# An adaptive-gate FFN with a quantised second layer on one core: GpSimd takes part of VectorE's and ScalarE's work, and the first FFN slots are put in a new order

## The chip, the cores and the metric

One core of one Trainium2 chip. The metric is the device time of one execution in microseconds. TensorE is called PE, VectorE DVE, ScalarE ACT, GpSimd POOL and SyncE SP below.

## The reference, cut to what matters

x holds 8 row blocks of 128 x 512 in float32. Layer 0 gates x and runs a ternary FFN on it; layer 1 multiplies by a weight that is first quantised with a codebook, and then by a base matrix with low-rank experts.

```python
y = einsum('bet,bt->be', x, mask) / length            # masked row means: x_sum, y_mean
g = x * sigmoid(conv5(y))                             # conv, y_safe, gates
aq = round(g * 127 / rowmax(|g|))                     # x_max, x_scales, x_quantise
wq(w) = clip(round(w / mean|w|), -1, 1) * mean|w|     # weight_sum, weight_total, ternary
h = silu(aq @ wq(w_gate).T) * (aq @ wq(w_up).T)       # gate_up, hidden_chunk
x = x + act_quant(h) @ wq(w_down).T                   # hidden_scale, down, residual
delta = lora_B @ lora_A * 0.5
q = codebook[searchsorted(thresholds, (weight + delta) / scale)]
w_eff = q * scale + delta                             # normalise, masks, codebook, value, w_eff
z = x @ w_eff.T
x = x + z @ W_base.T + b + sum_e alpha_e * (z @ A_e.T) @ B_e.T * 2
```

## The kernel before

Every engine has a program written out by hand; the order in it is the order on the engine, and counting semaphores join them. There is no scheduler.

**Codebook stage.** The 512 x 512 weight lies in four tiles of 128 rows (k = 0 to 3) in `cond`. ACT scales a tile by the inverse scale (`scaled_weight`, four instructions), DVE adds the low-rank delta (`normalise`), makes seven 0/1 tiles `w > threshold` (`masks`, 128 x 512 each), and PE multiplies each by a diagonal of codebook steps and adds them up in PSUM (`codebook`). DVE multiplies by the scale (`value`) and adds the delta again (`w_eff`, 128 x 512 from two SBUF tiles). PE then folds w_eff and W_base together into one matrix M: `fold(o, k)` adds row tile o's part of column block k to `bank_m[k]`, 16 folds in all, which end in `m_copy` on ACT.

**Weights of the FFN.** ACT sums |w| of each part that lands (`weight_sum`), PE adds over the partitions (`weight_total`), DVE turns it into a scale (`weight_scale`), ACT rounds a chunk of columns to int16 (`rounded_chunk`), DVE clips it to -1, 0 or 1 (`ternary_chunk`). There are three chunks of 464, 464 and 448 columns, for gate (i = 0) and up (i = 1). The down weight has five parts; ACT sums three and DVE two.

**Slots.** A loop b = 0 to 7 runs on PE, ACT and DVE. Slot b holds `gate_up(b, 0..2)`, the two products of row block b by a chunk; ACT makes silu of the first, DVE multiplies by the second (`hidden_chunk`: a product and a row maximum), then `hidden_scale` gives the factor hq(b). ACT rounds (`hidden_round`), SP transposes by DMA, ACT evacuates (`hidden_evacuate`), and `down(b)` multiplies two or three slots later; `residual(b)`, `x1_transposes(b)` and `x1_low(b)` follow. gate_up of chunk n needs hidden_chunk n - 2 done, which frees the bank. The row blocks form groups 0 to 1, 2 to 4 and 5 to 7: sums, the conv, gates and scales are made for a group at a time, inside the slots. `last_fold`, `b_rows` and the low part of `m_s` (DVE, line 1373) are small steps of layer 1 that `x1_transposes(0)` waits for in slot 3. Behind slot 7 comes layer 1 proper.

**Loads.** SP issues all of them in one order, first the head: 1060 columns of 4 bytes on 128 partitions, which hold the low-rank pair of layer 1's weight (1024 columns) and small numbers (codebook, lengths, active experts, log scales).

## Time and profile before

| | us |
|---|---|
| median of 3 runs | 153.93 (153.88 to 154.12) |
| the profiled execution | 153.92 |
| its span, first to last instruction | 152.1 |
| PE, DVE, ACT, POOL busy | 138.4, 114.1, 96.1, 11.0 |

Busy time is what an engine spent in instructions; matmuls overlap at their ends, so PE's is a little high. An instruction's cost on its engine is best read as the distance from its start to the next one's when nothing is waited for. A bracket at the end of a row gives the idle time ahead of it and what ended that. Idle time costs something only on the engine that the others wait for.

### The profile page before, as it was taken

Reading aid. Unit: us, or ns where it says so; the run is one execution under the profiler, and the core shown is the slowest. Engines: PE = TensorE matmul, PEld = TensorE weight load, DVE = VectorE, ACT = ScalarE, POOL = GpSimd, SP = SyncE. Lnnn points to the kernel's source line nnn. Section 1 sums busy time; section 2 is a strip of 40 time slices with the busy share of each in tenths; the row PEclk is TensorE's granted clock in tenths of the full one; section 3 lists DMA queues with packets and bytes.
Section 4 is the critical chain, followed back from the end, with each engine's and each line's share of the span. In section 5 each row is a group of like instructions: output and inputs, shape, how many; then the busy total and the mean of one; then the engine's idle time right before and its main releaser. Section 6 shows DMA issues by size and latency. Waiting matters only on the chain.

```text
span 152.1 us, 2134 instructions
## 1 busy us (share of the span) xinstructions
PE 138.4 (91%) x661; PEld 84.7 (56%) x661; DVE 114.1 (75%) x302; ACT 96.1 (63%) x156; POOL 11.0 (7%) x31
## 2 busy tenths in 40 slices
PE   6779999998799967898579999999999999999993
PEld 2256665753356544446234545454576766797792
...
DMA packets 19486, 19.22 MB, mean 126 GB/s; under 512 B 13474, under 2 KB 13858, under 8 KB 19476
## 3 DMA queue, kind: packets, MB, share of 16 engines
...
## 4 chain that ended last, share of the span: by engine, by line
PE 50%; DVE 27%; ACT 10%; issue 8%; DMA 2%; SPq 0%; ACTq 0%; DVEq 0%
PE bank L971 15%; PE bank L918 12%; ACT tern_d L526 6%; PE bank L881 6%; PE bank L887 6%; DVE hmax L1322 5%; DVE raw_gate L1319 4%; PE bank L929 3%; DVE junk L1158 2%; DMA cond<-in_cond_w 2%; DVE rmax L1208 2%; ACT cond L492 2%; PE bank L978 1%; DVE tern_i L1203 1%; PE bank L863 1%
## 5 line engine op out<-in xcount | busy, mean ns | idle before, releaser
L881 PE MATMUL bank<-tern_g,head_sb 128*128 128x464 bf16 (+1 forms) x96 | 22.6, 357 | 1.0 <-DVE tern_u L1204 0.8
L887 PE MATMUL bank<-tern_u,head_sb 128*128 128x464 bf16 (+1 forms) x96 | 22.5, 357 | 0.6 <-DVE raw_gate L1319 0.6
L918 PE MATMUL bank<-tern_d,delta 128*128 128x512 bf16 (+1 forms) x88 | 22.0, 399 | 0.5 <-DVE tern_d L1204 0.5
L971 PE MATMUL bank<-m_h,fr 128*128 128x512 f32 (+1 forms) x72 | 22.3, 378 | 0.0
L1319 DVE TENSOR_TENSOR raw_gate<-bank,wbt 128x464 f32<-128x464 f32 (+1 forms) x24 | 15.1, 631 | 4.2 <-ACT wbt L624 3.7
L624 ACT ACTIVATE wbt<-bank,s_g 128x464 f32<-128x464 f32 (+1 forms) x24 | 14.9, 633 | 3.4 <-PE bank L881 3.3
L1322 DVE TENSOR_REDUCE hmax<-raw_gate 128x1 f32<-128x464 f32 (+1 forms) x24 | 15.1, 631 | 0.8
L631 ACT ACTIVATE raw_gate<-raw_gate,hq 128x1376 int16<-128x1376 f32 x8 | 11.5, 1438 | 6.5 <-DVE hq L1329 6.5
L918 PEld LDWEIGHTS bank<-tern_d,delta 128*128 128x128 bf16 (+1 forms) x88 | 9.0, 103 | 11.5 <-issue 1.9
L887 PEld LDWEIGHTS bank<-tern_u,head_sb 128*128 128x128 bf16 x96 | 9.3, 98 | 10.0 <-DVE raw_gate L1319 1.2
L796 PE MATMUL bank<-wbt,cond 128*128 128x512 f32 x32 | 14.8, 599 | 0.0
L971 PEld LDWEIGHTS bank<-m_h,fr 128*128 128x128 f32 x72 | 13.2, 189 | 2.7
L785 PE MATMUL bank<-masks,diag_h 128*128 128x512 f32 x28 | 12.4, 444 | 1.9 <-DVE masks L1120 1.9
L881 PEld LDWEIGHTS bank<-tern_g,head_sb 128*128 128x128 bf16 x96 | 8.8, 101 | 8.8 <-DVE tern_u L1204 1.3
L971 PE MATMUL bank<-m_l,fr 128*128 128x512 f32 (+1 forms) x36 | 13.3, 370 | 0.0
L1120 DVE TENSOR_SCALAR masks<-cond,th 128x512 fp32r<-128x512 f32 x28 | 11.7, 483 | 0.2
L786 PE MATMUL bank<-masks,diag_l 128*128 128x512 f32 x28 | 11.1, 395 | 0.0
L1341 DVE TENSOR_TENSOR fr<-bank,fr 128x512 fp32r<-128x512 f32 x8 | 5.5, 692 | 7.2 <-ACT fr L658 7.0
L464 POOL TENSOR_SCALAR head_sb<-xs,gate,qx 128x512 int16<-128x512 f32 x6 | 5.4, 897 | 70.6 <-DVE qx L1224 69.2
L658 ACT ACTIVATE fr<-bank 128x512 fp32r<-128x512 f32 x8 | 4.7, 594 | 8.0 <-PE bank L929 8.0
L1432 DVE TENSOR_TENSOR xs<-bank,xs 128x512 f32<-128x512 f32 (+1 forms) x9 | 5.2, 625 | 5.8 <-PE bank L978 5.8
L796 PEld LDWEIGHTS bank<-wbt,cond 128*128 128x128 f32 x32 | 5.8, 190 | 5.5 <-issue 5.0
...
## 6 DMA issues: line engine op xcount, KB each, us to landing
...
```

The costliest lines, as they stand in the source:

```text
L624: act.activation(silu[:, n % 2, 0:w], bank_g[n % 2][:, 0:w], ACT.Silu, scale=s_g[:, b:b + 1]).then_inc(silu_done, 1)
L631: act.activation(h_i[:, b % 2, 0:F], hbuf[b % 2], ACT.Copy, scale=hq[:, b:b + 1]).then_inc(hint_done, 1)
L785: pe.matmul(bank_cb[k][:], diag_h[:, t, :], mask[i % SLOTS], start=(n == 0), stop=False)
L786: mm = pe.matmul(bank_cb[k][:], diag_l[:, t, :], mask[i % SLOTS], start=False, stop=(n == NT - 1))
L796: mm = pe.matmul(bank_m[k][:], cond[:, o, k * P:(k + 1) * P], wbt[:, o, :], start=(o == 0), stop=(o == KH - 1))
L881: mm = pe.matmul(bank_g[n % 2][:, 0:w], xq_t[:, b % 2, k, :], tern_g[:, k, f0:f0 + w], start=(k == 0), stop=(k == KH - 1))
L887: mm = pe.matmul(bank_u[n % 2][:, 0:w], xq_t[:, b % 2, k, :], tern_u[:, k, f0:f0 + w], start=(k == 0), stop=(k == KH - 1))
L918: mm = pe.matmul(bank_down[:], h_t[0:rows, b % 2, j, :], tern_d[0:rows, j, :], start=(j == 0), stop=(j == KF - 1))
L971: pe.matmul(bank_y[n_res][:, h0:h1], a[:, b, k, :], m[:, k, h0:h1], start=(n == 0), stop=False)
L1120: dve.tensor_scalar(mask[i % SLOTS], cond[:, k, :], t(T_ORDER[n]), None, ALU.is_gt)\
L1319: dve.tensor_tensor(hs, bank_u[n % 2][:, 0:w], silu[:, n % 2, 0:w], ALU.mult)\
L1322: link(dve.tensor_reduce(hmax[:, b % 2, c:c + 1], hs, AX.X, ALU.max, apply_absolute_value=True))
```

## The change

- **Head.** The small numbers (36 columns) become a transfer of their own, issued by ACT; the pair of 1024 columns stays first on SP's queue. The thresholds are put in order and the lengths and expert numbers made ahead of `normalise(0)`, which now waits for ACT's scaled groups one at a time.
- **GpSimd.** It scales tiles 1 to 3 (three 128 x 512 products, in place of twelve ACT instructions), makes all four `w_eff`, and for row blocks 5 to 7 makes the 0/1 mask and its product with x; ACT sums that product (`masked_sum`, at the end of slot 2). DVE's three `x_sum` of these blocks go.
- **Down weight.** DVE sums three parts instead of two.
- **Hidden scale.** The maxima of chunks 0 and 1 lie behind the hidden row, and the reduction of chunk 2 takes them in; the separate reduction goes.
- **Order.** The folds of tile 1 to 3 go from between the codebooks into the waits ahead of slot 0 and into slots 0 and 1; the ternary chunks are made as listed in ROUNDED, gate and up by turns; row block 2 is transposed by DMA, block 1 on PE ahead of slot 0. Only `m_copy` 3 and 2 are left; 1 and 0 stay in PSUM. Silu of chunk (b+1, 0) is issued in slot b for b up to 3. The weight total of the down weight goes behind gate_up(2, 1), selection_out ahead of hidden chunk (1, 2), and in slot 3 residual and m_s go ahead of hidden chunk (3, 1).

```diff
-X_BY_DMA = 3
+X_BY_DMA = 2
...
+ROUNDED = ((0, 0), (0, 1), (1, 0), (1, 1), (0, 2), (1, 2))
+SILU_TO = 4
+M_ORDER = (3, 2, 1, 0)
+M_COPIED = 2
...
-SUMMED_BY_ACT = 3
...
+SUMMED_BY_ACT = 2
...
-            sp.dma_start(head_sb[:], head).then_inc(ld_head, 16)
+            sp.dma_start(head_sb[:, 0:2 * H], lora0).then_inc(ld_lora, 16)
...
+            transpose_x(2)
             for b in range(NB):
                 if b < H_BY_DMA:
                     transpose_h(b)
-                if X_BY_DMA <= b + 3 < NB:
+                if b + 3 < NB:
...
+            def scaled_weight(k):
+                pool.wait_ge(inv_done, 1)
+                pool.wait_ge(ld_cond[k], 16)
+                v = cond[:, k, :].rearrange("p (g i) -> p g i", g=KH)
+                pool.tensor_tensor(v, v, scl_inv[:, k, :].unsqueeze(2).broadcast_to([P, KH, GROUP]),
+                                   ALU.mult).then_inc(condn_done, 1)
+
+            def w_eff(k):
+                pool.wait_ge(delta_done, min(k + 2, KH))
+                pool.wait_ge(value_done, k + 1)
+                pool.tensor_tensor(cond[:, k, :], cond[:, k, :], delta[:, k, :], ALU.add).then_inc(weff_done, 1)
+
+            def masked_x(b):
+                m = masked[:, b - GROUPS[2][0], :]
+                pool.wait_ge(ld_x[b], 16)
+                pool.wait_ge(len_done, 1)
+                pool.tensor_scalar(m, t_iota[:], len_f[:, b:b + 1], None, ALU.is_lt).then_inc(below_done, 1)
+                pool.wait_ge(below_done, b - GROUPS[2][0] + 1)
+                pool.tensor_tensor(m, m, xs[:, b, :], ALU.mult).then_inc(masked_done, 1)
+
+            for k in range(1, KH):
+                scaled_weight(k)
+            w_eff(0)
+            w_eff(1)
...
+            w_eff(2)
+            w_eff(3)
+            pool.wait_ge(cb_ps, KH)
+            for b in range(GROUPS[2][0], NB):
+                masked_x(b)
...
+            act.dma_start(head_sb[:, 2 * H:HEAD], head).then_inc(ld_head, 16)
...
-            scaled_weight(0)
+            act.wait_ge(inv_done, 1)
+            act.wait_ge(ld_cond[0], 16)
+            for g in range(KH):
+                c = slice(g * GROUP, (g + 1) * GROUP)
+                act.activation(cond[:, 0, c], cond[:, 0, c], ACT.Copy,
+                               scale=scl_inv[:, 0, g:g + 1]).then_inc(condn0_done, 1)
...
+            def masked_sum(b):
+                i = b - GROUPS[2][0]
+                act.wait_ge(masked_done, i + 1)
+                act.activation(masked[:, i, :], masked[:, i, :], ACT.Copy,
+                               accum_out=ysum[:, b:b + 1]).then_inc(xsum_done, 1)
...
             weight_sum_up(0)
             weight_sum_up(1)
+            conv_out(0)
             weight_sum_up(2)
+            gate_silu(0)
+            weight_sum_up(3)
             rounded_chunk(0, 0)
-            weight_sum_up(3)
             rounded_chunk(0, 1)
-            conv_out(0)
-            rounded_chunk(0, 2)
-            gate_silu(0)
+            x_evacuate(0)
+            x_evacuate(1)
             rounded_chunk(1, 0)
-            x_evacuate(0)
             rounded_chunk(1, 1)
...
+                if b == 2:
+                    for i in range(GROUPS[2][0], NB):
+                        masked_sum(i)
...
                 fold(0, k)
             codebook(2)
             weight_total(0, bank_total[0], KH)
-            for k in range(KH):
-                fold(1, k)
+            conv(0)
             codebook(3)
-            conv(0)
             weight_total(1, bank_total[1], KH)
-            for k in range(KH):
-                fold(2, k)
...
-            fold(KH - 1, 0)
-            fold(KH - 1, 1)
+            fold(1, 0)
+            fold(1, 1)
+            fold(1, 2)
             x_transposes(0)
-            fold(KH - 1, 2)
+            x_transposes(1)
+            fold(1, 3)
+            fold(2, 3)
+            fold(2, 2)
+            fold(2, 1)
             for b in range(NB):
                 gate_up(b, 0)
+                if b == 0:
+                    fold(3, 3)
+                    fold(3, 2)
+                    conv(1)
...
-                if b == 2:
-                    weight_total(2, bank_total[2], len(DOWN_PARTS))
                 if b == 3:
                     down(0)
                     last_fold(2)
+                    conv(2)
                     last_fold(3)
                 gate_up(b, 1)
-                if b == 3:
-                    conv(2)
...
                 if b == 2:
+                    weight_total(2, bank_total[2], len(DOWN_PARTS))
                     last_fold(0)
...
                     selection(KH)
+                    fold(2, 0)
+                    fold(3, 0)
...
-            def w_eff(k):
-                dve.wait_ge(delta_done, min(k + 2, KH))
-                dve.wait_ge(value_done, k + 1)
-                dve.tensor_tensor(cond[:, k, :], cond[:, k, :], delta[:, k, :], ALU.add).then_inc(weff_done, 1)
...
+            inner_thresholds()
+            lengths()
+            outer_thresholds()
+            adapter_numbers()
             normalise(0)
-            masks(0, 0, 1)
-            ordered_thresholds()
-            masks(0, 1)
+            dve.wait_ge(th_done, 2)
+            masks(0)
             normalise(1)
             masks(1, 0, 3)
             value(0)
             masks(1, 3)
-            w_eff(0)
             normalise(2)
+            selectors()
             value(1)
-            w_eff(1)
-            masks(2)
-            lengths()
+            masks(2, 0, 4)
+            x_sum(0)
+            masks(2, 4)
+            x_sum(1)
+            y_mean(0)
...
-                link(dve.tensor_reduce(hmax[:, b % 2, c:c + 1], hs, AX.X, ALU.max, apply_absolute_value=True))
+                if c < NC - 1:
+                    row_max, src = hrow[b % 2][:, F + c:F + c + 1], hs
+                else:
+                    row_max, src = hred[:, b:b + 1], hrow[b % 2][:, f0:F + NC - 1]
+                link(dve.tensor_reduce(row_max, src, AX.X, ALU.max, apply_absolute_value=True))
...
                 if b == 1:
-                    y_reciprocal(1)
-                    gates(1)
-                    x_scales(2, 5)
+                    weight_sum_down(2)
...
-                    x_max(5, NB)
                     residual(0)
+                    dve.wait_ge(msh_done, 1)
+                    dve.tensor_tensor(ms_l, bank_ms.rearrange("p (k c) -> p k c", k=KH),
+                                      ms_h.bitcast(F32), ALU.subtract).then_inc(msl_done, 1)
...
                 if b == 1:
+                    selection_out()
                     weight_sum_down(3)
+                if b < NB:
+                    if b == 0:
+                        y_reciprocal(1)
+                        gates(1)
+                        x_scales(1)
+                    hidden_chunk(b, 2)
+                    if b == 3:
+                        residual(1)
+                    hidden_scale(b)
+                if b == 1:
                     weight_sum_down(4)
-                if b < NB:
-                    hidden_chunk(b, 2)
-                    hidden_scale(b)
-                if b == 0:
-                    x_max(2, 5)
-                if b == 1:
                     weight_scale(2, bank_total[2])
-                    selection_out()
...
                     ternary_down(4)
-                    x_sum(5)
-                    x_sum(6)
-                    x_sum(7)
+                    dve.wait_ge(xsum_done, NB - GROUPS[2][0])
                     y_mean(2)
-                if b == 3:
-                    y_reciprocal(2)
-                    gates(2)
-                    x_scales(5, NB)
-                    x1_low(0)
-                if 3 <= b <= NB + 1:
+                    x_max(5, 6)
+                    x_max(6, 7)
```

GpSimd ahead of the slots, before: five iotas and small steps up to `fold_two` (line 444 on), then nothing until it quantises rows of x (line 464).

```order
L442 MEMSET ones 128x128
L444 TENSOR_SCALAR low_row<-part 128x1
L445 TENSOR_SCALAR tmp_row<-part 128x1
L447 TENSOR_TENSOR low_row<-low_row,tmp_row 128x1
L449 TENSOR_SCALAR sign_row<-low_row 128x1
L450 TENSOR_SCALAR two_row<-part 128x1
L453 TENSOR_SCALAR fold_two<-diff 128x36
L454 TENSOR_SCALAR fold_tmp<-diff 128x36
L456 TENSOR_TENSOR fold_two<-fold_two,fold_tmp 128x36
L464 TENSOR_SCALAR head_sb<-xs,gate,qx 128x512 x2
```

And now: the scalings (line 461), two w_eff (line 467), the same small steps, the other two w_eff.

```order
L455 MEMSET ones 128x128
L461 TENSOR_TENSOR cond<-cond,scl_inv 128x512 x3
L467 TENSOR_TENSOR cond<-cond,delta 128x512 x2
L482 TENSOR_SCALAR low_row<-part 128x1
L483 TENSOR_SCALAR tmp_row<-part 128x1
L485 TENSOR_TENSOR low_row<-low_row,tmp_row 128x1
L487 TENSOR_SCALAR sign_row<-low_row 128x1
L488 TENSOR_SCALAR two_row<-part 128x1
L491 TENSOR_SCALAR fold_two<-diff 128x36
L492 TENSOR_SCALAR fold_tmp<-diff 128x36
L494 TENSOR_TENSOR fold_two<-fold_two,fold_tmp 128x36
L467 TENSOR_TENSOR cond<-cond,delta 128x512 x2
```

The seven instructions on `cond` are new on this engine, and the small steps have moved behind five of them; the masks and products (lines 473 and 475) follow.

PE from the weight total of the up weight to slot 0's second chunk, before. `wbt,cond` are folds, `ident_b,head_sb` transposes of x, `tern_g` and `tern_u` the two halves of gate_up.

```order
L757 MATMUL bank<-wsum,ones 128x4
L796 MATMUL bank<-wbt,cond 128x512 x6
L853 MATMUL bank<-ident_b,head_sb 128x128 x4
L796 MATMUL bank<-wbt,cond 128x512
L881 MATMUL bank<-tern_g,head_sb 128x464 x4
L887 MATMUL bank<-tern_u,head_sb 128x464 x4
L881 MATMUL bank<-tern_g,head_sb 128x464 x4
L887 MATMUL bank<-tern_u,head_sb 128x464 x4
L796 MATMUL bank<-wbt,cond 128x512
L815 MATMUL bank<-ymean,band 128x3
L853 MATMUL bank<-ident_b,head_sb 128x128 x4
L881 MATMUL bank<-tern_g,head_sb 128x448 x4
```

And now, over the same stretch:

```order
L810 MATMUL bank<-wsum,ones 128x4
L849 MATMUL bank<-wbt,cond 128x512 x3
L901 MATMUL bank<-ident_b,head_sb 128x128 x8
L849 MATMUL bank<-wbt,cond 128x512 x4
L932 MATMUL bank<-tern_g,head_sb 128x464 x4
L938 MATMUL bank<-tern_u,head_sb 128x464 x4
L849 MATMUL bank<-wbt,cond 128x512 x2
L868 MATMUL bank<-ymean,band 128x3
L932 MATMUL bank<-tern_g,head_sb 128x464 x4
L938 MATMUL bank<-tern_u,head_sb 128x464 x4
L849 MATMUL bank<-wbt,cond 128x512
L932 MATMUL bank<-tern_g,head_sb 128x448 x4
```

Seven folds stand ahead of gate_up(0, 0) as before, but they are four of tile 1 and three of tile 2 in place of four of tile 2 and three of tile 3; both transposes come ahead of the last four; tile 3's first two folds stand behind gate_up(0, 0).

DVE from the end of slot 2 into slot 3, before. `xs<-bank` is residual(0), `m_s` the low part that x1_transposes(0) waits for.

```order
L1203 TENSOR_SCALAR tern_i<-raw_down,winv 96x512
L1204 TENSOR_SCALAR tern_d<-tern_i 96x512
L1158 SCALAR_TENSOR_TENSOR junk,ysum<-t_iota,len_f,xs 128x512 x3
L1163 TENSOR_TENSOR ymean<-ysum,len_r 128x3
L1319 TENSOR_TENSOR raw_gate<-bank,wbt 128x464
L1322 TENSOR_REDUCE hmax<-raw_gate 128x1
L1208 TENSOR_REDUCE rmax<-xs 128x3
L1336 SCALAR_TENSOR_TENSOR xs<-bank,s_d,xs 128x512
L1319 TENSOR_TENSOR raw_gate<-bank,wbt 128x464
L1322 TENSOR_REDUCE hmax<-raw_gate 128x1
L1373 TENSOR_TENSOR m_s<-bank,m_s 128x4x36
```

And now:

```order
L1262 TENSOR_SCALAR tern_i<-raw_down,winv 96x512
L1263 TENSOR_SCALAR tern_d<-tern_i 96x512
L1222 TENSOR_TENSOR ymean<-ysum,len_r 128x3
L1267 TENSOR_REDUCE rmax<-xs 128x1 x2
L1387 TENSOR_TENSOR raw_gate<-bank,wbt 128x464
L1394 TENSOR_REDUCE raw_gate<-raw_gate 128x1
L1408 SCALAR_TENSOR_TENSOR xs<-bank,s_d,xs 128x512
L1430 TENSOR_TENSOR m_s<-bank,m_s 128x4x36
L1387 TENSOR_TENSOR raw_gate<-bank,wbt 128x464
L1394 TENSOR_REDUCE raw_gate<-raw_gate 128x1
```

The three masked sums on `junk` are gone, two of the three maxima of x (`rmax`) stand ahead of the first hidden product, and `m_s` stands ahead of the second hidden product instead of behind it.

## Rows read from the trace of the kernel before

**Rows 1.** The page: shares of the span in the chain that ended last, by engine.

```profile
PE 50%; DVE 27%; ACT 10%; issue 8%; DMA 2%; SPq 0%; ACTq 0%; DVEq 0%
```

**Rows 2.** Busy time of each engine in three stretches, instructions in brackets; then clock, DMA.

```profile
50.00:55.00 5.00, 3.69 (x25) 2.48 (x24) 4.62 (x14) 4.29 (x8) 1.50 (x2) 1.00 0.38 72
75.00:80.00 5.00, 2.98 (x10) 1.56 (x11) 3.93 (x12) 2.56 (x5) 0.00 (x0) 0.72 0.00 0
90.00:95.00 5.00, 5.00 (x29) 2.75 (x28) 2.47 (x5) 5.00 (x9) 0.00 (x0) 1.00 0.41 79
```

**Rows 3.** VectorE's instructions in order of time, head and codebook stage.

```profile
1.09 0.23 DVE L1068 TENSOR_SCALAR ident<-diff 128x128 f32<-128x128 f32 x1
...
1.23 0.63 DVE L1069 TENSOR_SCALAR ident_b<-diff 128x128 bf16<-128x128 f32 x1
4.13 0.16 DVE L1073 TENSOR_REDUCE cbm<-head_sb 128x1 f32<-128x8 f32 x1 [2.26 <-DMA head_sb<-in_head]
...
6.29 1.13 DVE L1108 SCALAR_TENSOR_TENSOR cond<-bank,inv_part,cond 128x128 f32<-128x128 f32 x4 [0.45 <-ACT cond L492]
...
17.59 0.75 DVE L1128 SCALAR_TENSOR_TENSOR cond<-bank,cbn,scl 128x512 f32<-128x512 f32 x1 [0.16 <-DVE cond L1108]
18.45 0.69 DVE L1135 TENSOR_TENSOR cond<-cond,delta 128x512 f32<-128x512 f32 x1
19.05 2.86 DVE L1120 TENSOR_SCALAR masks<-cond,th 128x512 fp32r<-128x512 f32 x7
...
32.96 0.16 DVE L1169 TENSOR_TENSOR ytiny<-ycond 128x2 f32<-128x2 f32 x1 [0.36 <-ACT ycond L573]
```

**Rows 4.** VectorE's instructions in order of time, slots 0 to 2.

```profile
48.04 0.16 DVE L1326 TENSOR_REDUCE hred<-hmax 128x1 f32<-128x3 f32 x1
...
54.76 1.81 DVE L1308 TENSOR_REDUCE wsum<-raw_down 128x1 f32<-128x1024 f32 x2
...
60.68 0.94 DVE L1204 TENSOR_SCALAR tern_d<-tern_i 128x1536 bf16<-128x1536 int16 x1
61.54 0.62 DVE L1319 TENSOR_TENSOR raw_gate<-bank,wbt 128x464 f32<-128x464 f32 x1
...
62.87 0.56 DVE L1204 TENSOR_SCALAR tern_d<-tern_i 128x1536 bf16<-128x1536 int16 x1
...
69.73 0.75 DVE L1158 SCALAR_TENSOR_TENSOR junk<-t_iota,len_f,xs 128x512 f32<-128x512 f32 x1
...
70.53 0.75 DVE L1158 SCALAR_TENSOR_TENSOR junk<-t_iota,len_f,xs 128x512 f32<-128x512 f32 x1
```

**Rows 5.** The chain that ended last, in order of time: start us, us, what.

```profile
77.02 0.89 PE bank L929 x4
77.91 3.80 PE bank L918 x11
81.70 0.79 PE bank L881 x4
...
86.79 2.38 PE bank L918 x11
```

**Rows 6.** TensorE's instructions in order of time, gate_up(3,1).

```profile
71.01 0.95 PE L881 MATMUL bank<-tern_g,head_sb 128*128 128x464 bf16 x4
```

**Rows 7.** ScalarE's instructions in order of time, a copy and an accumulator read.

```profile
18.12 0.59 ACT L505 ACTIVATE delta<-bank 128x512 f32<-128x512 f32 x1
...
21.45 0.19 ACT L526 ACTIVATION_READ_ACCUMULATOR tern_d<-raw_gate 128x1 f32 x1
```

**Rows 8.** GpSimd's instructions in order of time.

```profile
1.23 0.56 POOL L441 IOTA t_iota<- 128x512 f32 x1
...
53.50 1.52 POOL L464 TENSOR_SCALAR head_sb<-xs,gate,qx 128x512 int16<-128x512 f32 x2 [49.24 <-DVE qx L1224]
...
59.66 1.54 POOL L464 TENSOR_SCALAR head_sb<-xs,gate,qx 128x512 int16<-128x512 f32 x1
```

**Rows 9.** The DMA issues by line: transposes of x rows, count and median us to landing.

```profile
raw_gate<-head_sb SPq DMA_TRANSPOSE x5, 2.8
```

204 lines of the change are left out of this document (109 added, 95 removed).

## The prediction

> **What bounds the kernel now.** I read the page first. The chain that ended last gives 50% of the span to TensorE (PE) and 27% to VectorE (DVE), so the bound changes hands [rows 1]. The table by stretches shows where. At 50 to 55 us DVE is busy 4.62 of 5 us and PE 3.69; at 90 to 95 us PE is busy all of it and DVE 2.47. At 75 to 80 us PE is busy 2.98 us at a mean granted clock of 0.72 of its full level, 2.4 GHz; the other two stretches are at 1.00 [rows 2]. So up to about 77 us the kernel runs at DVE's pace, behind that at PE's. The chain in order of time gives the hand-over: PE starts the transposes of slot 3 at 77.02, down(1) at 77.91 and gate_up(4,0) at 81.70 [rows 5]. From there 152.1 - 81.7 = 70.4 us are left, in which PE hardly waits and the change edits little; so the question is how early gate_up(4,0) can start. The profiled execution took 153.92 us around a span of 152.1; the median of the runs is 153.93, so nothing is to be corrected.
>
> I follow DVE from landmark to landmark, with the distance between two starts as the cost of an instruction.
>
> **First landmark, the hidden scale of row block 0.** Before, hq(0) is done at 48.7; behind it DVE still does the maxima, gates and scales of blocks 2 to 4. The changed order does these ahead of it, which moves work but adds none, so I compare the sums.
> - Head: DVE's first reading instruction waited 2.26 us until 4.13, for the whole head of 530 KB [rows 3]. Only the small numbers (18 KB) are needed there, now on a queue of its own. No row shows how soon 18 KB land beside the 512 KB that follow; the gain lies between 0 and the whole wait of 2.26, and I take the middle, 1.1 (DVE starts at 3.0).
> - Three DVE idles, 0.45 (ScalarE scaled four groups before DVE might start; now it starts after the first), 0.16 and 0.36 us [rows 3]: 0.97 gone. The thresholds and the lengths fill the time until the first scaled group.
> - w_eff: four additions go to GpSimd (POOL). One took 19.05 - 18.45 = 0.60 us of DVE's time [rows 3], so 2.4.
> - One reduction of a hidden scale (0.16 and 0.03 of gap) [rows 4]: 0.2.
> - Added: about 0.1 of waiting for the first silu.
> Sum 4.6: hq(0) at about 47.4 with the gates of blocks 2 to 4 already done, which before were done at 52.0 with their maxima (1.8) and scales (1.5). PE has to keep up. Laid out with its own distances in the new order, it runs through codebook(2), then waits some 1.6 us in codebook(3) for DVE's last masks, because the folds of block 1 that filled this place stand behind it; folds move into the wait for the ternary weights, and gate_up(0,0) comes at 36.3 instead of 38.6. Nothing on DVE waits longer for it. ScalarE (ACT) loses three scalings and two m copies, so its weight sums end about 3 us earlier and its rounding stays ahead of DVE. w_eff(3) is the latest of POOL's results: value(3) at 33, the sum at 34.5, its first fold at 38.
>
> **Second landmark, the start of slot 2 on DVE** (hidden product (2,0), 61.54 before [rows 4]). In slot 1 DVE gets one more weight sum. Parts 3 and 4 together took 1.81 us; a part of 1024 columns is 1.1 of that [rows 4]. Two new waits: selection_out now stands ahead of chunk 2, but PE's last selection comes behind gate_up(1,2) (PE at 51.55, DVE ready at 51.2: 0.35), and weight_scale(2) waits for the weight total that PE now multiplies only behind gate_up(2,1) (PE at 56.5, DVE ready at 55.65: 0.9). One reduction less, 0.2. Row block 2 now comes by DMA: POOL quantises it at 45.5 to 46.3, SP's transpose of it stands ahead of that of h(0), which is ready only at 48.8, and 2.8 us later [rows 9] it lies there, at 49.3 with its issue; gate_up(2,0) wants it at 53.1, so it costs nothing while POOL is less than 3.5 us late. The gain shrinks by 1.1 + 0.35 + 0.9 - 0.2 = 2.1, to 2.5 us: slot 2 starts at about 59.0.
>
> **Third landmark, the mean of blocks 5 to 7 and gate_up(3,1) on PE.** In slot 2 DVE is rid of three masked sums, 70.53 - 69.73 = 0.80 each, 2.4 us, and one reduction [rows 4]. It would reach the mean at 66.3. But ACT now sums, in order behind silu(3,0), the b rows and the evacuation of block 1. PE ends gate_up(3,0)'s first half near 63.1; silu 0.6, b rows 0.6, evacuation 1.5 take ACT to 65.8. A 128x512 ACT copy is 0.59 and the accumulator's read 0.19 [rows 7], 0.75 each with overlap: 68.1. So DVE waits 1.8 us at 66.3, what was won in this slot is mostly given back, and conv(2) and gate_up(3,1) on PE come at 69.2 instead of 71.01 [rows 6]. Gain 1.8.
>
> **Fourth landmark, gate_up(4,0).** Before, PE sat from 74.24 (71.01 and 3.23 for the conv and two chunks of gate_up) to 77.02, waiting for DVE's m_s low part; behind the wait the clock was down and down(1) took 3.80 instead of 2.38 [rows 5]. DVE had put a maximum of 1.8 us, a residual and a hidden chunk ahead of m_s. Now m_s comes ahead of the chunk, at about 71.6, while gate_up(3,2) runs until 72.3: the wait of 2.78 and the 1.42 of cold clock go. gate_up(4,0) at 69.2 + 1.57 + 1.54 + 0.89 + 2.38 = 75.6. Against 81.70 the gain is 6.1 us. DVE is then some 3 us further behind PE than before at this point, but the PE-bound slots leave it idle (2.47 us of work in 5 at 90 to 95 us [rows 2]), and hidden products are needed only two chunks later, so I charge nothing; if that cover fails it costs up to 1 us.
>
> **The price of GpSimd.** POOL gets three scalings, four w_eff and three pairs of mask and product, in place of nothing between 4.3 and 53.5 us. Its only rows of this size have one input: two took 1.52, so 0.76 each; the one at 59.66 took 1.54 [rows 8]. A two-input 128x512 is not in the trace. I bound it by 0.76 and 1.54. POOL itself has time: all is needed later than that. What matters is what POOL does to DVE. At 59.66 POOL's instruction met two DVE tensor_scalars, and the second took 0.94 us where the same form took 0.56 later; at 1.23 an iota of 0.56 met ident_b, 0.63 where its sister was 0.23 [rows 3, 4, 8]. So twice DVE lost 0.4 us to one POOL instruction. At 53.50 POOL ran beside DVE's hidden product, with one input in PSUM, and both kept their time [rows 8]. I count the meetings before slot 0 with DVE work of the first kind (masks, x_sum, ternary, small thresholds): two scalings (one hides under a normalise), four w_eff, three of the six masked pieces: nine. 9 x 0.4 = 3.6 us, all on DVE's path. Bounds: 0, and nine whole POOL instructions, 9 x 1.15 (the middle of 0.76 and 1.54) = 10.4.
> The Trainium skill (SBUF — State Buffer, Who interferes with whom) says that a VectorE instruction in a 2-port mode, or with two SBUF inputs against a reading GpSimd one, and the GpSimd instruction exclude each other for the whole instruction, the later one blocking fully. By that the sum would go to its upper bound, not to 3.6; the two sightings agree with blocking, but DVE lost less than POOL's whole time in both (0.38 of 0.77, 0.40 of 0.56). The same skill (GPSIMD Engine Reference, Elementwise) gives 4497 ns for a two-input add of 2048 columns, so by estimate some 1.2 us for 512; by it nine would be 10.8.
>
> **Sum.** 153.92 - 6.1 + 3.6 = 151.4 us.
>
> **Rivals.**
> - *GpSimd costs DVE nothing* (it gets in only beside normalise, value and reductions). For it: the pair at 53.50, and consumers that come late. Against: the two sightings. 147.8 us.
> - *GpSimd blocks DVE for its whole time.* For it: ident_b took most of the iota's time on top; DVE has few instructions here that would not meet it. Against: POOL waits too, and DVE queues its masks without a wait between. 147.8 + 10.4 = 158.2, slower. It decides from 6.1 us on, 0.68 us per meeting.
> - *PE's gaps move rather than vanish.* PE loses its steady supply at 23 to 28 us and at gate_up(2,2) (1.5 us for DVE's product); a lowered clock or a late masked sum gives back the 2.78 + 1.42 of slot 3: 151.4 + 4.2 = 155.6, or with half of it 153.5. For it: 2.6 us without work was enough at 75 us. Against: at 50 to 55 us PE was idle for 1.31 us at a clock of 1.00 [rows 2].
> - *The order does not change the bound*, no change: would need the above to cancel.
>
> **Numbers.** My forecast (losses of 1.5 to 6 us) 0.55, no cost 0.20, whole blocking 0.14, moved gaps 0.11. Faster by more than 0.2% (0.3 us, what a measurement of this kernel can tell) takes all of the second, nearly all of the first: 0.74. Slower takes whole blocking and over half of the gaps: 0.21. Same 0.05. The range 148.0 to 155.0 leaves out the lower part of the no-cost case and most of whole blocking.
>
> **What the profile would show.** Right: DVE's first codebook instruction near 3.0; hidden product (2,0) near 62.5 with the loss in; an ACT wait of DVE before the mean of blocks 5 to 7; no PE wait ahead of the slot 3 transposes, clock 1.00 there, down(1) at 2.4 us; mask and x_sum rows on DVE some longer than 0.40 and 0.75. Wrong: masks of 1.5 us each beside a POOL row; PE waits over 2 us in slots 2 to 4; a head that lands as late as before.

## The result, and the profile after

The changed kernel takes 165.34 us (median of 4 runs, 164.11 to 165.90) against 153.91 before: ratio 1.073, 95% interval 1.0668 to 1.0791. The forecast was 151.4 within 148.0 to 155.0. Two rivals named the right kind of loss, GpSimd blocking (158.2) and gaps of PE that move (155.6); both together are what happened, and more. The profiled run took 165.9 us around a span of 164.1. Executions more than 1.5% above the fastest of their own kernel are left out of every ratio and time below.

The page of the changed kernel, chain by engine (answers to [rows 1]), and then its table by stretches, in the columns of [rows 2]:

```profile
PE 69%; DVE 14%; issue 6%; DMA 6%; ACT 3%; ACTq 0%
```

```profile
5.00:10.00 5.00, 1.98 (x4) 0.68 (x4) 4.43 (x16) 4.48 (x17) 3.03 (x3) 1.00 1.03 392
10.00:15.00 5.00, 1.97 (x5) 1.61 (x6) 4.83 (x19) 2.54 (x7) 0.00 (x0) 0.64 1.04 417
50.00:55.00 5.00, 5.00 (x16) 2.38 (x15) 4.54 (x7) 3.89 (x5) 3.67 (x3) 0.77 0.00 0
75.00:80.00 5.00, 4.25 (x21) 2.32 (x21) 4.28 (x11) 2.92 (x6) 0.00 (x0) 0.88 0.00 0
```

PE's larger share of the chain is no sign of a fuller PE: it has a granted clock of 0.64 at 10 to 15 us and 0.77 at 50 to 55. It idles and then runs slowly. DVE, in the head (answers to [rows 3]), with POOL's row of the same time:

```profile
5.29 0.16 DVE L1128 TENSOR_REDUCE cbm<-head_sb 128x1 f32<-128x8 f32 x1 [3.42 <-DMA head_sb<-in_head]
...
7.04 0.95 DVE L1146 TENSOR_TENSOR th<-th 128x1 f32<-128x1 f32 x1
7.91 0.14 DVE L1147 TENSOR_TENSOR th<-th 128x1 f32<-128x1 f32 x1
7.98 1.02 DVE L1194 CAST act_f<-head_sb 128x4 f32<-128x4 int32 x1
8.91 0.16 DVE L1195 CAST len_f<-head_sb 128x8 f32<-128x8 int32 x1
9.10 0.89 DVE L1196 TENSOR_SCALAR act_n<-act_f 128x4 f32<-128x4 f32 x1
...
11.23 0.35 DVE L1169 SCALAR_TENSOR_TENSOR cond<-bank,inv_part,cond 128x128 f32<-128x128 f32 x1
```

```profile
6.93 3.03 POOL L461 TENSOR_TENSOR cond<-cond,scl_inv 128x512 f32<-128x512 f32 x3 [4.92 <-DMA cond<-in_cond_w]
```

The small numbers came 1.16 us later than in [rows 3], not earlier. Three instructions that need 0.15 us took about a microsecond, one for each of POOL's three scalings. The first normalise starts at 11.23 (6.29 before), and PE has idled 5.93 us when it gets the first mask:

```profile
13.03 0.77 PE L838 MATMUL bank<-masks,diag_h 128*128 128x512 f32 x1 [5.93 <-DVE masks L1181]
...
83.76 0.95 PE L932 MATMUL bank<-tern_g,head_sb 128*128 128x464 bf16 x4
...
86.85 0.60 PE L980 MATMUL bank<-ident,xs 128*128 128x128 f32 x4
87.28 2.54 PE L968 MATMUL bank<-tern_d,delta 128*128 128x512 bf16 x10
89.66 0.95 PE L932 MATMUL bank<-tern_g,head_sb 128*128 128x464 bf16 x4
...
93.09 0.96 PE L938 MATMUL bank<-tern_u,head_sb 128*128 128x464 bf16 x4 [0.92 <-DVE raw_gate L1387]
...
104.66 0.93 PE L932 MATMUL bank<-tern_g,head_sb 128*128 128x448 bf16 x4 [2.02 <-ACT wbt L673]
```

These rows answer to [rows 5, 6]. gate_up(3,1) comes at 83.76 (71.01 before). From it to gate_up(4,0), at 89.66, PE takes 5.90 us instead of 10.69: the wait for m_s and the cold down(1) are gone, as forecast. But gate_up(4,0) is 7.96 us later than before, and what follows loses another 4.0: in slots 4 and 5 new waits stand (0.92, 0.48 and 2.02 us).

### The profile page after: what moved, and what is told of

It reads as the page before. It is cut to its first block, busy times and chain, and to the rows that moved or that the text cites. A ratio compares the mean times of both kernels' runs of the same rounds, so it can differ in the third digit from the quotient of the medians.

```text
span 164.1 us, 2122 instructions
## 1 busy us (share of the span) xinstructions
PE 141.3 (86%) x652; PEld 86.6 (53%) x657; DVE 117.0 (71%) x287; ACT 92.5 (56%) x146; POOL 30.7 (19%) x44
## 4 chain that ended last, share of the span: by engine, by line
PE 69%; DVE 14%; issue 6%; DMA 6%; ACT 3%; ACTq 0%
PE bank L1022 14%; PE bank L968 10%; PE bank L938 9%; PE bank L932 9%; PE bank L849 7%; DVE masks L1181 4%; PE bank L838 3%; DMA raw_gate<-raw_gate 3%; PE bank L839 3%; DMA head_sb<-in_head 3%; PE bank L980 2%; PE bank L875 2%; PE bank L1029 1%; DVE cond L1169 1%; PE bank L911 1%
## 5 line engine op out<-in xcount | busy, mean ns | idle before, releaser
L938 PE MATMUL bank<-tern_u,head_sb 128*128 128x464 bf16 (+1 forms) x96 | 23.8, 373 | 2.3 <-DVE raw_gate L1387 2.3
L838 PE MATMUL bank<-masks,diag_h 128*128 128x512 f32 x28 | 13.6, 485 | 9.3 <-DVE masks L1181 9.3
L968 PE MATMUL bank<-tern_d,delta 128*128 128x512 bf16 (+1 forms) x83 | 19.4, 379 | 1.0 <-ACT b_full L760 0.8
L849 PE MATMUL bank<-wbt,cond 128*128 128x512 f32 x32 | 16.1, 639 | 0.0
L1181 DVE TENSOR_SCALAR masks<-cond,th 128x512 fp32r<-128x512 f32 x28 | 12.7, 517 | 0.2
L838 PEld LDWEIGHTS bank<-masks,diag_h 128*128 128x128 f32 x28 | 6.2, 222 | 12.5 <-issue 8.4
L839 PE MATMUL bank<-masks,diag_l 128*128 128x512 f32 x28 | 12.4, 443 | 0.0
L512 POOL TENSOR_SCALAR s_d<-harow,w 128x1 f32<-128x1 f32 x8 | 3.1, 384 | 42.2 <-DVE hq L1401 31.0
L1394 DVE TENSOR_REDUCE raw_gate<-raw_gate 128x1 f32<-128x464 f32 x16 | 10.2, 636 | 0.5
L467 POOL TENSOR_TENSOR cond<-cond,delta 128x512 f32<-128x512 f32 x4 | 5.2, 1298 | 24.9 <-DVE cond L1189 13.1
```

The costliest lines, as they stand in the source:

```text
L838: pe.matmul(bank_cb[k][:], diag_h[:, t, :], mask[i % SLOTS], start=(n == 0), stop=False)
L839: mm = pe.matmul(bank_cb[k][:], diag_l[:, t, :], mask[i % SLOTS], start=False, stop=(n == NT - 1))
L849: mm = pe.matmul(bank_m[k][:], cond[:, o, k * P:(k + 1) * P], wbt[:, o, :], start=(o == 0), stop=(o == KH - 1))
L938: mm = pe.matmul(bank_u[n % 2][:, 0:w], xq_t[:, b % 2, k, :], tern_u[:, k, f0:f0 + w], start=(k == 0), stop=(k == KH - 1))
L968: mm = pe.matmul(bank_down[:], h_t[0:rows, b % 2, j, :], tern_d[0:rows, j, :], start=(j == 0), stop=(j == KF - 1))
L1181: dve.tensor_scalar(mask[i % SLOTS], cond[:, k, :], t(T_ORDER[n]), None, ALU.is_gt)\
```

## The experiments

All differences are against the kernel before on the same chip (153.6 to 154.0 us there). "Position of DVE" is the start of the row that writes qx of blocks 5 to 7, read from the profile of each run.

**1. The changed kernel, taken apart.** *order_only* has the new order and the split head, and none of the GpSimd work:

```
-  POOL: scaled_weight(1..3), w_eff(0..3), masked_x(5..7)
+  ACT: scaled_weight(1..3), placed as before;  DVE: w_eff(0..3), x_sum(5..7)
```

> The changed kernel with all of GpSimd's new work taken back: scalings on ScalarE, w_eff and the masked sums on VectorE; new order and split head stay. Theory 1, the shared port: in the changed kernel's trace nine or so VectorE instructions beside a GpSimd one are longer by 0.4 to 1.1 us, some 8 us in all, and TensorE's first codebook ran 2.5 us longer at the lowered clock behind the wait this made; VectorE gets 2.4 us of w_eff back, and the 2.9 us wait for ScalarE's sums turns into 2.4 us of work: 165.3 - 8 - 2.5 + 2.4 - 0.5 = 156.7, still slower than before by the later head (1.1) and what slots 4 and 5 lose. Rival, the new order is what costs: the time stays above 161.

158.6 us (157.54 and 159.67, with 160.29 and 161.31 left out; too much spread for a ratio). Neither number was met: of the 11.4 us about 6.7 go with GpSimd, and 4.7 stay with order and head. Its trace shows PE waiting 1.35 us at gate_up(2,2) and 1.06 for the mean, then a clock of 0.51 at 75 to 80 us.

*scale_on_act* puts back the three scalings alone:

```
-  POOL: scaled_weight(1..3)
+  ACT: scaled_weight(1) among the diagonals, (2) and (3) around delta_out
```

> The changed kernel with only the three scalings back on ScalarE at their former places. Theory 1: the three short VectorE instructions of 0.95, 1.02 and 0.89 us fall to 0.15 (2.5 us), the TensorE wait ahead of the first mask falls from 5.9 to about 3.4 us, and some of the cold-clock 2.5 us goes: 160 to 163. Rival, the head and the thresholds ahead of normalise(0) make that wait: 164.5 or more.

160.55 us (159.83 and 161.27; 162.38 is left out, and so is the profiled run, which was disturbed); ratio 1.0432 [1.0365, 1.0499]. By the ratios the scalings cost 4.6 us, with some 1.5 of uncertainty; the expected 160 to 163 was met.

*one_head* has the head as one transfer again:

```
-  sp.dma_start(head_sb[:, 0:2 * H], lora0);  act.dma_start(head_sb[:, 2 * H:HEAD], head)
+  sp.dma_start(head_sb[:], head)
```

> The changed kernel with the head in one transfer on SyncE's queue again. If the second queue delays both, as the trace suggests (the small head landed at 5.3 us, the pair at 5.1, where the whole had landed by 4.13), every step comes 1.1 us earlier: 164.2. If the late landing is chance or hidden: no change within 0.3 us. If the small part is really sooner in some executions: slower.

163.57 us, ratio 1.0619 [1.0565, 1.0673]: 1.8 us less, where 1.1 was expected.

*silu3* changes one number, so that ACT does silu(4,0) in slot 4 and not ahead of the high part of x1(0):

```
-  SILU_TO = 4
+  SILU_TO = 3
```

> The changed kernel with silu of chunk (4, 0) issued in slot 4 as before, one number (SILU_TO 4 to 3). Theory: in slot 3 it stands on ScalarE ahead of the high part of x1 of block 0 and waits for TensorE's gate_up(4, 0); VectorE's low part waits behind that for 1.6 us, with hidden product (3, 2) and the hidden scale of block 3 behind it, which makes h(3) late for slot 5. TensorE's waits of 0.9, 0.5 and 2.0 us in slots 4 and 5 go: 162.0. Rival, the masked sums and the late slot 3 make them: within 0.5 us of 165.3.

161.57 us (165.03 left out), ratio 1.0506 [1.0459, 1.0553]: 3.4 us less by the ratios. Only some 1.1 of that lies behind DVE's position (span less position is 73.3 us, against 74.4 in the changed kernel and 70.6 before). The rest came earlier in the program, where the edit moves nothing: in that profile the head landed at 4.63, not 5.29, and other stretches were the cold ones. So a profile of this kernel can differ from its sister by 2 us before the first hidden product (48.34 against 50.33), and I rest no size on a single total.

**2. GpSimd against the undisturbed kernel.** *before_six_adds* puts the disputed cost into the kernel before and nothing else (the later writers of m_l and m_h wait for the additions, which are long done):

```
+  pool.wait_ge(value_done, 1)
+  for i in range(6):        # results are never read
+      pool.tensor_tensor(dst[:, i % KH, :], t_iota[:], t_iota[:], ALU.add)
```

> The kernel before, with six two-input 128x512 additions on POOL behind value(0), beside DVE's masks of codebooks 1 and 2. Their results are overwritten by later writes and nobody reads them; nothing else is changed. If a meeting costs DVE about 0.9 us, as the changed kernel's rows suggest: +5.4, so 159.3 us. At the 0.4 us of the prediction: +2.4, 156.3. If POOL only takes what DVE leaves: 153.9. In the trace the masks beside a POOL row should take 1.3 us instead of 0.40 by the first, 0.8 by the second.

156.65 us, ratio 1.0181 [1.0148, 1.0214], +2.7. The profile, POOL and then DVE:

```profile
14.41 4.75 POOL L461 TENSOR_TENSOR m_l<-t_iota 128x512 fp32r<-128x512 f32 x4 [10.15 <-DVE cond L1134]
19.13 2.48 POOL L461 TENSOR_TENSOR m_h<-t_iota 128x512 fp32r<-128x512 f32 x2
```

```profile
14.25 4.02 DVE L1126 TENSOR_SCALAR masks<-cond,th 128x512 fp32r<-128x512 f32 x4
18.19 1.52 DVE L1141 TENSOR_TENSOR cond<-cond,delta 128x512 f32<-128x512 f32 x1
19.64 1.12 DVE L1114 SCALAR_TENSOR_TENSOR cond<-bank,inv_part,cond 128x128 f32<-128x128 f32 x4
20.79 0.75 DVE L1134 SCALAR_TENSOR_TENSOR cond<-bank,cbn,scl 128x512 f32<-128x512 f32 x1
```

An addition takes 1.19 to 1.24 us. Four masks take 1.0 us each instead of 0.40, the w_eff addition 1.52 instead of the usual 0.69. The normalise and the value, whose one input is in PSUM, keep their 1.12 and 0.75 beside POOL. So the price is 0 for one kind of instruction and 0.6 to 0.83 for the other. The average over the six is 0.45 because the last two met mostly the first kind, and because DVE, 3.2 us late behind them (its next w_eff starts at 21.64 instead of 18.45), made up 0.45 of that by its position.

*before_weff* moves the four w_eff additions alone:

```
-  DVE: w_eff(0..3)
+  POOL: w_eff(0..1); its row steps; w_eff(2..3)
```

> The kernel before, with only the four w_eff additions moved from DVE to POOL. DVE is rid of 4 x 0.60 = 2.4 us. At 0.9 us a meeting it loses 3.6: 153.9 - 2.4 + 3.6 = 155.1 us. At the predicted 0.4 it loses 1.6: 153.1.

154.62 us, ratio 1.004 [1.0011, 1.0068]: between the two, 0.7 us slower although DVE is rid of 2.4. The clearest meeting of all is here, POOL first:

```profile
34.69 1.28 POOL L447 TENSOR_TENSOR cond<-cond,delta 128x512 f32<-128x512 f32 x1 [5.34 <-DVE cond L1138]
```

```profile
34.66 0.16 DVE L1174 TENSOR_TENSOR ytiny<-ycond 128x2 f32<-128x2 f32 x1
34.86 1.14 DVE L1175 TENSOR_SCALAR ytiny<-ytiny 128x2 f32<-128x2 f32 x1
```

Two elements per partition take 1.14 us instead of 0.17: DVE's instruction starts 0.17 us behind POOL's and ends at 36.00, as POOL's does at 35.97. The length of the DVE instruction doesn't matter, only what is left of POOL's. Of the four additions one met no such instruction; beside the other three DVE's rows are 1.01, 0.53 and 0.97 us longer, 2.5 in all, which cancels the 2.4 that DVE was rid of.

*before_scale* moves the three scalings alone:

```
-  ACT: scaled_weight(1..3)
+  POOL: scaled_weight(1..3), ahead of its row steps
```

> The kernel before, with only the scaling of weight columns 1 to 3 moved from ACT to POOL (three instructions with a broadcast, near 1.0 us each in the changed kernel). At 0.9 us a meeting and three meetings with thresholds, normalise and masks: 153.9 + 2.7 = 156.6 us, and a PE that waits longer for the first masks. At the predicted 0.4 and two meetings: 154.7; no change if ACT's relief pays for it.

156.48 us, ratio 1.0179 [1.0146, 1.0212], +2.5; the clock is 0.66 at 10 to 15 us, PE having waited 1.43 us for a mask. Only 1.1 us of the loss stands in longer DVE rows (a mask, 0.74 instead of 0.49, and a 128x1 threshold, 0.99 instead of 0.15).

*before_masked* moves the masked sums of blocks 5 to 7 alone:

```
-  DVE, slot 2: x_sum(5); x_sum(6); x_sum(7)
+  POOL, once the codebook is done: masked_x(5..7);  ACT, slot 2: masked_sum(5..7)
```

> The kernel before, with only the masked sums of blocks 5 to 7 moved: mask and product on POOL behind the last codebook, the three sums on ACT behind the evacuation of h(1) in slot 2, DVE waiting for them ahead of the mean. DVE is rid of 2.4 us in slot 2 and waits for ACT some of it back; POOL's six instructions run beside ternary, x_sum and maxima. At 0.9 us for each of the three or four that meet SBUF-to-SBUF work, +3, less 1 for what the wait leaves: about 156. At the prediction's 0.4: 153.9 - 0.6 + 1.2 = 154.5. If the pieces hide: 153.3.

157.36 us, ratio 1.0225 [1.0184, 1.0266], +3.7: worse than either forecast. DVE and PE in its profile, then the table of its stretches:

```profile
38.81 1.55 DVE L1257 TENSOR_SCALAR head_sb<-xs,gate,qx 128x512 int16<-128x512 f32 x1
```

```profile
40.42 0.61 PE L879 MATMUL bank<-ident_b,head_sb 128*128 128x128 bf16 x4 [3.09 <-DVE head_sb L1257]
40.82 2.02 PE L822 MATMUL bank<-wbt,cond 128*128 128x512 f32 x2
42.63 1.75 PE L907 MATMUL bank<-tern_g,head_sb 128*128 128x464 bf16 x4
```

```profile
40.00:45.00 5.00, 4.58 (x13) 1.95 (x14) 4.80 (x12) 2.90 (x4) 0.09 (x1) 0.50 0.06 13
```

The quantising of row block 0 took 1.55 us (0.55 before), PE had waited 3.09 us for it and then ran at a clock of 0.50, half of its full level, so 1.2 GHz: gate_up(0,0) took 1.75 us for what takes 0.95. The loss of a meeting is paid twice, once on DVE and once in PE's clock: DVE in turn waits 1.03 us for PE ahead of its first hidden product (46.04).

**3. The order without GpSimd.** *order_clean* is order_only with one_head and silu3:

> The changed kernel without any of its GpSimd work (scaling on ACT, w_eff and the masked sums on DVE), with the head in one transfer as before, and with silu(4,0) behind silu(4,2)'s old place (SILU_TO = 3). So what is left is the new order of folds, chunks, sums, gates and transposes. The order with the split head and SILU_TO = 4 took 160.0. If the head and the silu of slot 4 cost what their single changes gave (1.8 and 3.4 us): 154.8 us. If the order itself loses time by a PE that runs dry and then cold in slots 2 and 3: 158 or more.

156.44 us, ratio 1.0181 [1.0149, 1.0213]: between. In its profile PE waits again in slot 4:

```profile
85.00 1.44 ACT L682 ACTIVATE raw_gate<-raw_gate,hq 128x1376 int16<-128x1376 f32 x1 [2.78 <-DVE hq L1409]
86.35 1.17 ACT L675 ACTIVATE wbt<-bank,s_g 128x464 f32<-128x464 f32 x2
```

ACT waits 2.78 us for hq(3), and silu(4,1) stands behind. *order_scale3* puts hidden_scale(3) straight behind its chunk, ahead of these:

```
   hidden_chunk(3, 2)
+  hidden_scale(3)
   x_max(7, NB) ... x_scales(2);  x1_low(0);  residual(1)
-  hidden_scale(3)
```

> The new order without GpSimd work, head in one transfer, SILU_TO = 3 (156.4 us), with hidden_scale(3) on DVE straight behind hidden_chunk(3, 2) as before, ahead of the last maximum, the scales of blocks 5 to 7, x1_low(0) and residual(1). In the parent's trace hq(3) came at 84.8, ACT's rounding of h(3) stood behind it and silu(4, 1) behind that, and PE waited 1.81 us at 87.0. If that stall comes from the place of hidden_scale(3): 1.8 us less, 154.6. If ACT is late for another reason, or the delayed x1_low(0) stops PE's transposes instead: 156.4.

156.02 us (154.87 to 156.57), ratio 1.0112 [1.0048, 1.0176]. The wait moved: PE now waits 1.37 us for residual(1) at 84.52 and 1.00 at 93.64. *order_scale3_sum2* gives the weight sum of part 2 back to ACT and puts the total and selection_out where they were:

```
-  DVE, slot 1: weight_sum_down(2);  PE, slot 2: weight_total(2) behind gate_up(2, 1)
+  ACT, slot 1: weight_sum_down(2);  PE, slot 2: weight_total(2) ahead of gate_up(2, 1)
```

> As order_scale3, with ACT summing part 2 of the down weights again (DVE is rid of one reduction of 1.1 us), selection_out behind weight_scale(2) and PE's weight total ahead of gate_up(2, 1), all as before. In the parent DVE waited 1.12 us for the total, PE 1.35 at gate_up(2, 2), and the clock then fell to 0.66 of full for some 5 us. If those are the price: 1.1 + 1.6 less than order_scale3, 152. If slots 0 to 2 run no earlier: no change against order_scale3.

156.07 us, ratio 1.0126 [1.0069, 1.0183]: no change; that theory fell. *gpsimd_clean* is order_scale3 with all GpSimd work:

> The changed kernel with all its GpSimd work, but with the three repairs of order_scale3 (one head transfer, SILU_TO = 3, hidden_scale(3) straight behind its chunk). order_scale3 took 156.0. If GpSimd's price is the same as between the changed kernel and order_only (165.3 - 160.0): 161.3. If it is the 8 us by which DVE rows were longer in the changed kernel's trace, nothing of it hidden: 164. At the prediction's 3.6: 159.6.

160.42 us (159.61 and 161.23; 162.92 and 163.26, the profiled run, are left out), ratio 1.0444 [1.0374, 1.0514]: 5.1 us above order_scale3 by the ratios, give or take 1.5. With it the loss has three measured steps, by the ratios and 154 us: 1.7 (order), 5.1 (GpSimd), 4.4 (split head and the two places in slots 3 and 4).

**4. What bounds the kernel up to slot 4.** *before_slot3* makes only the move from which the forecast had most of its gain (and, on ACT, puts the high part of m_s ahead of the evacuation of conv(2)):

```
   hidden_chunk(3, 0)
-  x_max(5, NB);  residual(0);  hidden_chunk(3, 1);  m_s low
+  residual(0);  m_s low;  hidden_chunk(3, 1)
   hidden_chunk(3, 2);  hidden_scale(3)
+  x_max(5, NB)
```

> The kernel before, with only slot 3 in another order: residual(0) and m_s's low part ahead of hidden_chunk(3, 1) on DVE, the maximum of blocks 5 to 7 behind hidden_scale(3), and on ACT m_s's high part ahead of the evacuation of conv(2). If the 2.78 us that PE waited for m_s and the 1.42 us of cold clock behind it go, as the prediction said, and the later maximum is hidden: 149.7 us. If DVE's deferred 1.8 us come back as waits for x1_low(0) in slot 4: about 151.5 to 152. No change if DVE bounds slot 4 as well.

153.87 us (155.97 left out), ratio 0.9996 [0.9969, 1.0022]: no change. PE in its profile:

```profile
74.39 0.60 PE L929 MATMUL bank<-ident,xs 128*128 128x128 f32 x4
74.83 2.54 PE L918 MATMUL bank<-tern_d,delta 128*128 128x512 bf16 x10
77.21 0.95 PE L881 MATMUL bank<-tern_g,head_sb 128*128 128x464 bf16 x4
...
83.25 0.66 PE L929 MATMUL bank<-ident,xs 128*128 128x128 f32 x4 [2.75 <-DVE xs L1336]
```

The wait for m_s and the cold down(1) of [rows 5] are gone and gate_up(4,0) comes 4.5 us earlier, as predicted. One slot later PE waits 2.75 us for residual(1), and at gate_up(6,0) it is 0.3 us ahead of before. DVE's row explains it: 81.65 against 81.50 in the profile before.

```profile
81.65 0.16 DVE L1224 TENSOR_SCALAR qx<-qx 128x3 f32<-128x3 f32 x1
```

DVE had the same amount of work up to there, in another order. *before_slot3_fold*, *before_fold* and *before_fold_sum3* therefore take work away: the row maxima folded into the third chunk's reduction (0.2 us a slot), then also part 3 of the down weights summed by ACT (1.2 us).

```
-  hmax(c) <- reduce(h chunk c);  hred <- reduce(hmax 128x3)
+  row(c) <- reduce(h chunk c), c < 2;  hred <- reduce(h chunk 2 and row(0..1))
   and in the two kernels with sum3:
-  DVE, slot 1: weight_sum_down(3)
+  ACT, slot 1: weight_sum_down(3), behind x_evacuate(2)
```

> As before_slot3, with the row maxima of the first two chunks kept beside h, so that the third chunk's reduction gives the row's maximum and the small reduction (0.16 us and its gap, once per slot) is gone. DVE bounds slots 0 to 3, so 0.2 us each: 0.8 us less than before_slot3. If DVE is not the bound there: no change.

152.71 us (155.22 left out), ratio 0.9933 [0.9901, 0.9965].

> The kernel before, with only the row maxima folded into the third chunk's reduction: one small reduction (0.16 us and its gap) less on DVE in each slot. If DVE's amount of work until the scales of blocks 5 to 7 bounds the kernel: 4 x 0.2 = 0.8 us less, 153.1. If gate_up(4,0) bounds it by way of the m_s low part: the same 0.8. If slots run at PE's pace: no change.

152.62 us, ratio 0.9925 [0.9899, 0.995]. That is 1.3 us, more than the 0.8 expected; DVE's position is 0.66 earlier, and down(1) runs at the full clock, 2.54 us, behind a PE wait of 1.51 instead of 2.62.

> As before_fold, with part 3 of the down weights summed by ACT in slot 1 (behind x_evacuate(2), 1.25 us where ACT later waits 1.97 us) instead of DVE (1.2 us). If DVE's amount of work until 82 us is the bound: 1.1 us less than before_fold, 152.0. If ACT's later h(0) or the weight total stops another engine: no better than before_fold.

152.13 us (151.43 to 153.23), ratio 0.9884 [0.9832, 0.9936]: the fastest kernel of the study, 1.2% ahead of before. DVE's position is 79.72.

> As before_fold_sum3, with slot 3 in the new order (m_s ahead of hidden_chunk(3, 1), the last maximum behind hidden_scale(3)). If DVE's amount of work is the bound, the order within slot 3 changes nothing again: the time of before_fold_sum3 within 0.3 us, near 152.0, though gate_up(4,0) comes some 4 us earlier. If the early gate_up(4,0) is worth something once DVE has less to do: 151 or less.

153.07 us, ratio 0.9927 [0.9891, 0.9964]: with slot 3 in the new order it is no better, though gate_up(4,0) comes at 77.02 against 78.28. Here PE met a clock of 0.66 at 55 to 60 us behind a wait of 1.13, and DVE waited 1.60 us for the weight total, so this pair doesn't isolate slot 3 cleanly.

Over fourteen kernels the span less DVE's position is nearly constant, in us: before 152.1 - 81.50 = 70.6; before_fold 150.6 - 80.84 = 69.8; before_fold_sum3 69.9; before_slot3 70.3; before_slot3_fold_sum3 70.4; before_slot3_fold 70.7; before_head 70.1; order_scale3 153.1 - 82.65 = 70.5; order_scale3_sum2 70.4; before_weff 70.0; before_scale 70.7; before_masked 155.7 - 85.89 = 69.8; before_six_adds 70.7; gpsimd_clean 161.5 - 91.25 = 70.3. Their spans reach from 149.6 to 161.5. Above it stand only the kernels with the changed slots 3 and 4: order_clean 73.3, silu3 73.3, the changed kernel 164.1 - 89.69 = 74.4, one_head 74.7, order_only 76.4. But in these five the row itself stands elsewhere: ahead of hidden_chunk(3, 2) and hidden_scale(3), which in the fourteen are done before it. The start of residual(1), behind hidden_chunk(3, 2) in all of them, compares more fairly. Here it is, before and in the changed kernel:

```profile
81.50 0.16 DVE L1224 TENSOR_SCALAR qx<-qx 128x3 f32<-128x3 f32 x1
82.30 0.74 DVE L1336 SCALAR_TENSOR_TENSOR xs<-bank,s_d,xs 128x512 f32<-128x512 f32 x1
```

```profile
89.69 0.17 DVE L1280 TENSOR_SCALAR qx<-qx 128x3 f32<-128x3 f32 x1
...
91.81 0.69 DVE L1413 TENSOR_TENSOR fr<-bank,fr 128x512 fp32r<-128x512 f32 x1 [1.56 <-ACT fr L707]
...
93.72 0.75 DVE L1408 SCALAR_TENSOR_TENSOR xs<-bank,s_d,xs 128x512 f32<-128x512 f32 x1
```

The span less this start is 68.9 to 69.9 us in the fourteen and 70.4 to 71.0 in the five. In the changed kernel residual(1) starts 11.4 us later than before, nearly the whole loss.

*before_head* splits only the head:

```
-  sp.dma_start(head_sb[:], head)
+  sp.dma_start(head_sb[:, 0:2 * H], lora0);  act.dma_start(head_sb[:, 2 * H:HEAD], head)
```

> The kernel before, with only the head split: lora factors first on SP's queue, the 18 KB of small numbers on ACT's. The prediction had it at -1.1 us (DVE starts at 3.0 instead of 4.13). The changed kernel's trace had DVE start at 5.29, 1.16 later, the run without GpSimd work at 4.1. If the two transfers hinder each other: +0.5 to +1.1, 154.5 to 155.1, and more spread from run to run. If the small one lands early: 152.9.

154.07 us, ratio 1.0009 [0.9999, 1.002]. The small part reached DVE at 4.80, 0.67 later than the whole head before, and cost nothing by the end. Over the profiles with the split head it was there at 4.03, 4.63, 4.80 and 5.29; with one transfer at 4.08 to 4.33 over fifteen. (The disturbed profile of scale_on_act, also split, had it at 3.96.)

## Why the prediction was wrong

**The size of the miss.** The sum was 153.92 - 6.1 + 3.6, and both terms failed. By the ratios GpSimd adds 5.1 us net while DVE is rid of 2.4 us of w_eff, so its price is 7.5 instead of 3.6. The gain of 6.1, which held those 2.4, turned into a loss of 11.2 - 7.5 = 3.7: without w_eff and the head 2.6 were forecast for the order and 1.7 were lost, and the head's 1.1 became 4.4 of loss together with the two places in slots 3 and 4. This split follows the order in which the pieces were put in; how they act on each other wasn't measured apart.

**The price of GpSimd.** The prediction put "nine meetings" at 0.4 us, 3.6 in all, because two sightings of [rows 3, 8] showed 0.4. Measured, it is 7.5 (gpsimd_clean less order_scale3, and the 2.4), 0.83 for each of the nine, inside the bounds of 0 and 10.4 and in their upper half. The rows of the changed kernel say the same: those of DVE that overlap one of POOL's ahead of 56 us are 7.9 us longer than the same forms alone, 2.4 beside the scalings (0.80, 0.86, 0.72), 3.6 beside w_eff (0.57, 1.01, 0.96, 1.03) and 2.0 beside the masks and products. What misled me: in the two sightings only 0.52 us (59.66 + 1.54 - 60.68) and 0.56 us of POOL's instruction were left when the DVE instruction met it, and I read the 0.38 and 0.40 as a part of POOL's whole time (for the first I even took 0.77 as the whole, where its row says 1.54). A blocked instruction loses about what is left of the other (0.38 of 0.52, 0.40 of 0.56, and 0.97 of 1.11 in before_weff), so a late or short meeting is a lower bound for an early one. The Trainium skill (SBUF — State Buffer, Who interferes with whom) says that the later one blocks fully, that a DVE reduction on trn2 never contends, and that one SBUF input outside the two-port modes doesn't either. The trace agrees at each point that it shows: 1.14 us for two elements, 1.12 and 0.75 unchanged with a PSUM input, and in the changed kernel a reduction of 128x1536 that keeps the 1.75 us of before beside two POOL rows:

```profile
50.85 1.55 POOL L473 TENSOR_SCALAR raw_down<-t_iota,len_f 128x512 f32<-128x512 f32 x1
52.49 1.27 POOL L475 TENSOR_TENSOR raw_down<-raw_down,xs 128x512 f32<-128x512 f32 x1
```

```profile
51.67 1.75 DVE L1267 TENSOR_REDUCE rmax<-xs 128x3 f32<-128x1536 f32 x1
```

The rival with whole blocking stood at 158.2; it deserved the larger chance.

**That a filler costs nothing.** "The thresholds and the lengths fill the time until the first scaled group" failed twice. These small instructions were just those that stood beside POOL's scalings: 0.95, 1.02 and 0.89 us. And without GpSimd they weren't free either: the wait that they should fill was 0.45 us, but in order_scale3, with the head at 4.13 as before, they keep DVE from 5.88 to 7.71, and the first mask comes at 8.88 instead of 7.45.

**The head, -1.1.** Wrong in sign in the changed kernel: 5.29 against 4.13, 1.8 us by one_head. In the kernel before the same split changes nothing. Why the small transfer's arrival varies wasn't settled; no run here separates it from the transfers that start beside it.

**Slot 1 and slot 2.** The waits came as predicted: 1.10 us for selection_out (0.35 was the forecast) and 1.12 for the weight total (0.9). DVE's wait for the masked sums ended at 82.41 and was 2.88 us, where 1.8 was the forecast. But the second landmark, 59.0 and 62.6 with the price in, was reached at 72.22. The order without GpSimd had it at 62.88 and 62.99 (order_only, order_scale3; 61.54 before), and that is near what the forecast gives without w_eff's 2.4 and the head's 1.1, 62.5. The same holds for hq(0), 50.9 by that account and 51.03 to 51.20 in three profiles (52.36 in order_clean). So DVE's way through the order was followed about rightly.

**Slot 3.** The local mechanism was right twice: in the changed kernel and in before_slot3 PE's wait of 2.78 and the cold clock went.

**"The question is how early gate_up(4,0) can start"** is the step of the reading that failed. That stretch of 70.4 us was PE-bound only as long as DVE was no later, and the prediction saw DVE "some 3 us further behind PE" and charged nothing, at most 1. The runs show that it costs all of the gain (before_slot3: 4.5 us won at gate_up(4,0), 0 in the end). order_scale3 shows it again: gate_up(4,0) comes at 79.85, 1.85 us earlier than before and where the forecast has it without GpSimd and the head (79.7), yet its span is 1.0 us longer. PE's wait for m_s and DVE's work up to residual(1) were two chains of nearly the same length; shortening one shows the other. In the changed kernel two more things were late there, silu(4,0) ahead of x1_high(0) on ACT and hidden_scale(3) behind residual(1) on DVE. The first shows as DVE's wait of 1.56 us ahead of residual(1), which silu3 doesn't have; the second comes before PE's wait of 2.02 us for a silu in slot 5. Behind the start of residual(1) all this costs 70.4 less 69.8 us, the value before.

**Gaps of PE** were a rival with 0.11. They came everywhere: as a consequence of the GpSimd price (before_masked, 3.09 us and a clock of 0.50), and without GpSimd too (order_only, 1.35 and 1.06 us and a clock of 0.51). They were no alternative to the price but an addition.

What stays open: order_scale3 is 2.0 us slower than before (1.7 by the ratio), its profiled execution only 1.0, with DVE's position 1.15 us later (82.65 against 81.50). DVE starts the first hidden product of slot 0 together with before (41.84 in both) and those of slots 1, 2 and 3 later by 0.7, 1.5 and 2.7 us, in part because other work now stands ahead of them. Which step loses the time wasn't isolated; returning one weight sum did not bring it back.
